# An expert layer's second bias: added by GpSimd to the block's rows instead of as a product on TensorE

## The reference, cut to what matters

```python
logits = xf @ gate_w                               # xf: layer-normed rows, 2048 x 256; 8 experts
top_w, top_idx = jax.lax.top_k(logits, TOP_K)      # TOP_K = 2
top_w = jax.nn.softmax(top_w, axis=-1)
combine = zeros((t, e)).at[arange(t)[:, None], top_idx].add(top_w)
h = jax.nn.gelu(jnp.einsum('td,edf->tef', xf, w1) + b1, approximate=False)   # f = 1024
y = jnp.einsum('tef,efd->ted', h, w2) + b2
out = jnp.einsum('ted,te->td', y, combine)
return x + out
```

## Time and profile before

| | |
|---|---|
| median of 3 runs | 340.61 us (339.21 to 341.54) |
| the profiled execution | 339.56 us, of which the trace's span is 337.7 us |
| TensorE busy | 310.3 us, 92% of the span |
| VectorE, ScalarE, GpSimd busy | 255.1, 234.3 and 173.4 us |
| products of the bias, L1261 | 39 |
| fetches L498 and stores L505 | 39 each |

### The profile page before, as it was taken

How to read it: one execution, slowest core, us unless ns; L and a number is a source line. 1 busy time by engine, 2 the same in 40 slices (tenths; PEclk the granted TensorE clock), 3 DMA queues, 4 the chain that set the end, 5 groups by cost and what they waited for, 6 DMA issues and landing times.

```text
span 337.7 us, 11884 instructions
## 1 busy us (share of the span) xinstructions
PE 310.3 (92%) x4065; PEld 286.4 (85%) x4065; DVE 255.1 (76%) x577; ACT 234.3 (69%) x537; POOL 173.4 (51%) x189
## 2 busy tenths in 40 slices
PE   7688898999899998999999999999999999999960
PEld 4678787898788897998999999999999999999950
DVE  8799998877878978786877778878777766666620
ACT  1589898982626787877778878788788665656530
POOL 6978989974142353534444444444444444443311
PEclk9999999999979999999999999999999999999995
DMA  7999999999610297888787877897879788888321
GB/s 245 289 380 337 328 353 357 327 395 364 239 39 14 47 299 205 236 233 264 185 265 204 258 219 231 245 262 213 246 231 243 232 233 237 225 256 225 95 31 16
DMA packets 49219, 78.56 MB, mean 233 GB/s; under 512 B 12117, under 2 KB 25625, under 8 KB 47114
## 3 DMA queue, kind: packets, MB, share of 16 engines
q1 hardware_dynamic: 39208, 66.72, 55.4%
q0 software_dynamic: 7600, 10.48, 20.2%
q10 hardware_dynamic: 2354, 0.59, 0.8%
HBM read 31.07 MB, written 9.64 MB: 121 GB/s over the span
## 4 chain that ended last, share of the span: by engine, by line
PE 67%; DVE 7%; issue 4%; DMA 3%; POOL 2%; ACT 1%; POOLq 1%; DVEq 0%; ACTq 0%
PE bank L1244 27%; PE bank L1259 26%; PE bank L1188 2%; PE bank L1047 2%; PE bank L1088 1%; DMA shared<-xn_rows,row_of 1%; DVE shared L1003 1%; PE bank L1106 1%; DMA out<-shared,row_of 1%; PE bank L1261 1%; DVE W L954 1%; PE bank L1063 1%; PE bank L1097 1%; PE bank L1175 1%; PE bank L1202 1%
## 5 line engine op out<-in xcount | busy, mean ns | idle before, releaser
L1259 PE MATMUL bank<-W,shared 128*128 (+1 forms) x936 | 108.7, 273 | 0.7 <-DVE shared L1026 0.7
L1244 PE MATMUL bank<-shared,XR 128*128 128x128 f16 x1680 | 99.5, 219 | 2.0 <-issue 1.8
L1244 PEld LDWEIGHTS bank<-shared,XR 128*128 128x128 f16 x1680 | 96.1, 98 | 3.9 <-issue 3.4
L1259 PEld LDWEIGHTS bank<-W,shared 128*128 128x128 f16 x936 | 89.9, 98 | 10.8 <-issue 1.1
L498 POOL DMA_INDIRECT shared<-xn_rows,row_of x39 | 40.9, 1049 | 91.0 <-DVE w_of L1019 72.2
L505 POOL DMA_INDIRECT out<-shared,row_of x39 | 61.8, 1584 | 49.9 <-ACT shared L658 27.4
L649 ACT ACTIVATE shared<-shared 128x512 f32<-128x512 f32 x78 | 49.0, 628 | 47.0 <-DVE shared L1003 33.6
L1026 DVE SCALAR_TENSOR_TENSOR shared<-shared,XP 128x512 f16<-128x512 f32 x70 | 52.3, 748 | 25.9 <-ACT shared L651 13.8
L1003 DVE SCALAR_TENSOR_TENSOR shared<-bank,XP 128x512 f32<-128x512 f32 x70 | 52.4, 748 | 20.2 <-PE bank L1244 11.9
L651 ACT ACTIVATE shared<-shared,XP 128x512 f16<-128x512 f32 x70 | 50.5, 722 | 2.3
L954 DVE SCALAR_TENSOR_TENSOR W<-W,wscale (+1 forms) x32 | 40.9, 1281 | 2.2 <-issue 1.5
(11 more groups left out here) (179 smaller groups left out, 389.2 us busy)
## 6 DMA issues: line engine op xcount, KB each, us to landing
XR<-W SPq DMA_DIRECT2D x140, 256.0 KB
W<-in_w SPq DMA_DIRECT2D x16, 1024.0 KB, 8.1
shared<-in_ctx_t SPq DMA_DIRECT2D x16, 256.0 KB, 4.8
W<-in_ctx SPq DMA_DIRECT2D x16, 128.0 KB, 6.1
out<-XR SPq DMA_DIRECT2D x16, 128.0 KB, 6.3
xn_rows<-W SPq DMA_DIRECT2D x16, 128.0 KB, 6.7
XR<-in_x SPq DMA_DIRECT2D x3, 512.0 KB, 6.2
shared<-xn_rows,row_of POOLq DMA_INDIRECT x39
```

Source lines behind the costliest of these rows:

```text
L1244: mm = pe.matmul(pHT[n][m][:, f % 4, :], first[:, c, w, f * P:(f + 1) * P], XT[:, n, v, c, :], start=(c == 0 and w == 0 and v == 0), stop= ...
L1259: pe.matmul(pY[n], hT[:, n, v, f, :], whole(Wh[:, slot, at:at + D]), start=(f == 0 and w == 0 and v == 0), stop=False)
```

## The change

Three things. The second biases no longer pass through TensorE: for each block SyncE loads the expert's bias row, repeated over 128 partitions in DRAM (`b2_rows`, 128 KB), into `XB[:, b % 3]`. GpSimd multiplies it by the token weight and by the expert's scale, which is now a 19th parameter (`YSC`), into `term`, and adds `term` to `Y` ahead of the store. To know the expert of each block, the steps are taken for a second table `expert`, beside `wslot`. `B2`, `B2s`, `y_scale` and ScalarE's `biases` are gone; `BP` holds the attention's row alone. And `keep_busy` behind the table runs 28 products, no longer 38.

```diff
+            def load_bias(b):                                   # SyncE
+                e = bass.ds(sp.value_load(expert[0:1, b:b + 1], min_val=0, max_val=E - 1), 1)
+                after(sp, term_ok, b - 2)
+                sp.dma_start(XB[:, b % 3, :], b2_rows[e].rearrange("e p d -> p (e d)")).then_inc(xb_in[b % 3], 16)
...
+            sp.wait_ge(expert_ok, 1)
+            for b in range(3):
+                load_bias(b)
             for b in range(4, NB):
...
                     sp.wait_ge(pick_ok, b - 2)
+                    sp.wait_ge(term_ok, b - 2)
                 sp.dma_start(XP[:, b % 3, :], slot_par[:, s, :].rearrange("p a x -> p (a x)")).then_inc(par_in[b % 3], 16)
+                if b == 4:
+                    load_bias(3)
+                load_bias(b)
...
             for i in range(-2, NB + 2):                         # GpSimd
                 b = i + 2
...
                         .then_inc(xg_ok[b % 3], 16)
+                b = i
+                if 0 <= b < NB:
+                    pool.wait_ge(xb_in[b % 3], 16 * (b // 3 + 1))
+                    pool.wait_ge(got_w, b + 1)
+                    if b < 4:
+                        pool.wait_ge(param_ok, 1)
+                    else:
+                        pool.wait_ge(par_in[b % 3], 16 * par_uses(b))
+                    after(pool, sum_ok, b - 2)
+                    pool.tensor_scalar(term[:, b % 3, :], XB[:, b % 3, :], w_of[:, b:b + 1], params_of(b)[:, YSC:YSC + 1],
+                                       ALU.mult, ALU.mult).then_inc(term_ok, 1)
                 b = i - 2
                 if 0 <= b:
+                    pool.wait_ge(ys_ok, b + 1)
+                    pool.wait_ge(term_ok, b + 1)
+                    pool.tensor_tensor(Y[:, b % 2, :], Y[:, b % 2, :], term[:, b % 3, :], ALU.add).then_inc(sum_ok, 1)
                     after(pool, added, 16 * b)
-                    pool.wait_ge(ys_ok, b + 1)
+                    pool.wait_ge(sum_ok, b + 1)
                     pool.indirect_dma_start(out=out,
...
-            def biases(src, dst):                               # ScalarE
-                act.activation(B2s[0:3, dst, :], B2[0:3, src, :], ACT.Copy, scale=y_scale[0:3, src]).then_inc(b2_ok, 1)
...
-            dve.memset(B2[:, :, :], 0.0).then_inc(bias_zero, 1)
-            dve.memset(B2s[:, :, :], 0.0).then_inc(bias_zero, 1)
+            dve.memset(BP[:, :], 0.0).then_inc(bias_zero, 1)
...
+                beside(dve.tensor_tensor(step_e[:, 2, 0:E - 1], permf[:, 2:E + 1], permf[:, 1:E], ALU.subtract))
...
+                for n in range(2):
+                    dve.tensor_scalar(passed[:, n, :], iotaB128[:, :], step_p[:, 0:1], step_p[:, n + 1:n + 2],
+                                      ALU.is_ge, ALU.mult).then_inc(passed_ok, 1)
...
+                        dve.tensor_scalar(wslot[:, :], pSlot[:, 0, :], float(SPARE), None, ALU.add).then_inc(wslot_ok, 1)
+                        dve.tensor_scalar(expert[:, :], pSlot[:, 1, :], permf[:, 1:2], None, ALU.add).then_inc(expert_ok, 1)
...
-            keep_busy(pIdle, 38)                                # TensorE
+            keep_busy(pIdle, 28)
...
-                    pe.wait_ge(b2_ok, min(b // 4 + 1, E))
...
-                    pe.matmul(pY[n], ones3[:, :], B2s[:, slot, :].rearrange("p a d -> p (a d)"),
-                              start=False, stop=True).then_inc(y_ok, 1)
+                    mm.then_inc(y_ok, 1)
```

More of the change, by code:

```diff
@@ L23, in after, with xattn_moe_kernel @@
         eng.wait_ge(sem, value)
-def xattn_moe_kernel(nc, x, ctx_in, ctx_t, q_rows, ck, vcol, bias9, gate, w1, b1x, w2, out):
+def xattn_moe_kernel(nc, x, ctx_in, ctx_t, q_rows, ck, vcol, bp_row, b2_rows, gate, w1, b1x, w2, out):
     T, _, D = x.shape
@@ L102, in xattn_moe_kernel @@
         CX = early(NV, D)
-        bias_rows = early(D)[0:E + 1]
-        bias_rest = early(D)[0:E + 1]
-        bias_part = early(3 * D // 2)[0:E + 1].bitcast(BF16).rearrange("e (r d) -> e r d", r=3)
+        bias_rows = early(D)[0:1]
+        bias_rest = early(D)[0:1]
+        bias_part = early(3 * D // 2)[0:1].bitcast(BF16).rearrange("e (r d) -> e r d", r=3)
         GROUP = 8
@@ L160, in xattn_moe_kernel @@
         notri = sb("notri", [P, P], BF16)
+        term = sb("term", [P, 3, D])
         ones3 = sb("ones3", [P, P], BF16)
-        B2 = sb("B2", [P, E + 1, D], BF16)
-        B2s = sb("B2s", [P, E + 1, D], BF16)
+        BP = sb("BP", [P, D], BF16)
+        XB = sb("XB", [P, 3, D])
         GW = sb("GW", [P, C, E])
@@ L201, in xattn_moe_kernel @@
         ends = sb("ends", [P, E])
-        step_e = sb("step_e", [P, 2, E])
-        step_p = sb("step_p", [P, 2])
-        passed = sb("passed", [P, NB])
+        step_e = sb("step_e", [P, 3, E])
+        step_p = sb("step_p", [P, 3])
+        passed = sb("passed", [P, 2, NB])
         wslot = sb("wslot", [P, NB], I32)
+        expert = sb("expert", [P, NB], I32)
         tv = sb("tv", [P, NB])
@@ L263, in xattn_moe_kernel @@
         v_ok, ohr_ok, table_mm, tok_ok = sem("v_ok"), sem("ohr_ok"), sem("table_mm"), sem("tok_ok")
-        passed_ok, slot_mm = sem("passed_ok"), sem("slot_mm")
+        passed_ok, slot_mm, expert_ok = sem("passed_ok"), sem("slot_mm"), sem("expert_ok")
         perm_ok, wslot_ok, comb_ok, comb_out = sem("perm_ok"), sem("wslot_ok"), sem("comb_ok"), sem("comb_out")
         comb_step, den_ok = sem("comb_step"), sem("den_ok")
-        high_ok, low_ok, param_ok, b2_ok = sem("high_ok"), sem("low_ok"), sem("param_ok"), sem("b2_ok")
+        high_ok, low_ok, param_ok = sem("high_ok"), sem("low_ok"), sem("param_ok")
+        xb_in = [sem(f"xb_in{n}") for n in range(3)]
+        term_ok, sum_ok = sem("term_ok"), sem("sum_ok")
         gelu_set = sem("gelu_set")
@@ L1085, in attended @@
                         pe.wait_ge(bias_placed, 16 * 3)
-                    pe.matmul(pO, ones3[:, :], B2[:, E, :], start=True, stop=False)
+                    pe.matmul(pO, ones3[:, :], BP[:, :], start=True, stop=False)
                     for h in range(NH):
@@ L1210, in first_of_block_0 @@
                         mm.then_inc(h_ok, 1)
-                pe.wait_ge(passed_ok, 1)
-                pe.matmul(pSlot, ones32[:, :], passed[:, :], start=True, stop=True).then_inc(slot_mm, 1)
+                pe.wait_ge(passed_ok, 2)
+                pe.matmul(pSlot, ones32[:, :], passed[:, :, :], start=True, stop=True).then_inc(slot_mm, 1)
             for i in range(-1, NB + 1):
```

30 lines of the change are left out of this document (11 added, 19 removed).

## The result

The changed kernel takes 395.41 us (median, 395.09 to 406.75), beside 341.08 us for the kernel before in the same runs: 1.160 times as long (95% interval 1.154 to 1.166). Single executions of every kernel now and then run some per cent longer at a lower granted clock, here the one of 406.75; they are left out of all ratios. The forecast was 364, range 346 to 384: slower, as forecast, but by 54 us where 25 were forecast. The profiled execution took 395.52 us (span 393.7); it is compared with before's (339.56, span 337.7).

The account below looks back on a forecast made before the run. TensorE was full; the change makes it wait on GpSimd's fetch chain, 9.28 us plus 3.5 landing, 12.8 per two periods. With start and tail, +24.7 us on 339.56 gives 364, range 346 to 384.

Parts of the forecast that it names:

- The order of GpSimd's queue: GpSimd, from w_of to the next fetch: term, addition and store now stand between, 4.72 us forecast, 0.75 before.
- The two-period sum, its first term: T(k), TensorE starting block k+1's transposes, to w_of(k) written: 4.56 us of a chain of 12.8 per two periods.
- L, the landing of the fetch: From the start of GpSimd's fetch until its rows are in: 3.5 us taken, bounds 2.8 and 4.8.
- The waits: TensorE at L1188 waits for fetched rows in nearly every mid-loop block, 0.5 to 1.3 us; period 6.1 to 6.7.
- The start: Block 0's term waits for `expert` and its load; block 3's fetch starts at 111.7, T(2) about 114.7, 3.1 us later.
- The tail: Last additions stand between ScalarE's rows and the stores: one addition and its gaps, 0.8 us, on the path.
- L1261: The 39 bias products removed from TensorE: 3.8 to 4.2 us in all, while TensorE is what ends last.
- Ten unread products: Fewer on TensorE behind the table: 0.1 to 0.6 us gained, 0.3 taken, as block 0's transposes need a fetch.
- SyncE and the DMA engines: Added 128 KB load per block: 0.8 to 1.0 us on SyncE against 1.1 of waiting; DMA 5.1 of 6.4 us.
- The first: Rival: fetches stay in time and TensorE remains the bound, 337 us; chance 0.09.
- The second: Rival: DMA engines become the bound and weights land late, period near 5.7, about 343 us; chance 0.06.
- The third: Rival: GpSimd and the fetch are slower beside VectorE, period 7.1, about 388 us; chance 0.12.

Follow-up runs that it names:

- Experiment 1: Changed kernel with GpSimd's term taken for block i-1 in iteration i, no longer block i: 351.35 us, 1.032 of the kernel before.
- experiment 3: Kernel before with only GpSimd's wait for w_of(i) put ahead of its store, no term, addition or load: 348.07 us, 1.022.
- experiment 6: Kernel before with TensorE's register load of the weights' slot moved ahead of the wait for fetched rows: 338.22 us, 0.992.
- Experiment 2: Changed kernel with TensorE's register load of the weights' slot moved ahead of the wait for fetched rows: 379.37 us, 1.114 of the kernel before.
- Experiment 7: Kernel before without the 39 bias products L1261, second biases left out: 338.54 us, 0.994.
- experiment 4: Kernel before with 28 unread products behind the table in place of 38: 339.33 us, 0.999.
- experiment 13: Changed kernel with bias rows loaded for blocks 0 to 2 only: 394.41 us, 1.162 of the kernel before.
- experiments 9 and 10: Changed kernel, term of block i-1, register load ahead, without GpSimd's arithmetic: 9 keeps SyncE's loads, 351.33 us; 10 has loads for three blocks only, 335.23.
- experiment 11: Changed kernel, term of block i-1, register load ahead, loads for three blocks; GpSimd's arithmetic behind the store, addition to an unread tile: 339.28 us, 0.994.

## Why the prediction was wrong

The sign, the chain and the place of the first wait were right. By the prediction's own steps:

*The order of GpSimd's queue.* Right. w_of to fetch is 4.60 (4.72 was forecast), partly by luck: the single costs were off in ways that cancel. The costliest groups of the changed kernel (count, busy us, mean ns):

```profile
L1053 DVE SCALAR_TENSOR_TENSOR shared<-shared,XP 128x512 f16<-128x512 f32 x70 | 60.4, 863 | 25.6 <-ACT shared L675 25.4
L528 POOL TENSOR_SCALAR term<-XB,w_of,XP 128x256 f32<-128x256 f32 x35 | 30.9, 883 | 54.3 <-issue 53.6
...
L534 POOL TENSOR_TENSOR shared<-shared,term 128x256 f32<-128x256 f32 x39 | 30.0, 769 | 0.0
```

The term takes 883 ns (0.65 us was taken, below the 0.74 of the prediction's own slope and without a reason), the addition 769 (0.70), but the last gap 0.30 us (0.75). Experiment 1 undoes the order and takes 44 us; experiment 3 shows a part of it with the wait alone.

*The two-period sum, its first term.* This step failed. "T(k) to w_of(k), 4.56 us" was read in a block in which TensorE had not waited, and used for the blocks that wait. Behind a wait it is 5.71, and 5.67 in the mean of 15, and the trace of before had shown why: the wait at 128.82 is followed by a product only at 129.98 (experiment 6). While TensorE still works on older products, the register load behind them is hidden; when it has nothing left, 0.6 to 1.1 us are on the path. Experiment 2 takes it out: 16 us in all, 14 of them between T(4) and T(36). That stretch takes 226.2 us instead of the forecast 202.4 (14.1 a pair instead of 12.8): 23.8 of the 31 us that the forecast lacked.

*L, the landing of the fetch.* Mis-sized by less: 3.66 in the block shown, 3.92 in the mean of the 15 pairs (3.3 to 5.2), where 3.5 was taken. Over the loop that is some 6 us of the 23.8.

*The clock.* The prediction had no term for it. Three stretches of 3.4 us at half clock can cost the loop 5 us at most (an estimate: what is done in them would have taken half the time at the full clock); no experiment takes them out alone, and in experiment 2 two are left.

*The waits.* "Nearly every block, 0.5 to 1.3 us" did not come: every second block waits, for longer, and the periods alternate instead of lying between 6.1 and 6.7.

*The start.* T(2) was right to 0.1 us, by luck: the fetch started at 110.97 and not at 111.7, took 1.78 us to issue instead of 0.99, and was in after 3.66 us, where the forecast left 3.0. The products behind T(2) at half clock were not seen, and T(4) is 1.65 late.

*The tail.* "0.8 on the path" was mis-sized: 5.5. The addition was costed, and not that the term of block 38 keeps back the store of block 36, so that two stores instead of one run one behind the other. The forecast for T(37) to the end was 25.56 + 0.8 - 0.3 = 26.1, measured 31.1.

The sum of the misses: 1.65 + 23.8 + 0.6 (the last period) + 5.0 = 31 us, and 362.4 + 31.1 = 393.5, measured 393.7.

*L1261.* 4.2 us were counted. Experiment 7 gives 2.2, since TensorE was nearer to its chain than the profile's full 40 us let one think. It made no difference to this result.

*Ten unread products.* 0.3 us was taken; experiment 4 can tell no difference (0.997 to 1.002), nor could it tell 0.3 from nothing.

*SyncE and the DMA engines.* "It stays in time" held in the changed kernel (37.5 us of waiting for TensorE in 23 blocks, experiment 13) for a reason that was not given: the blocks had become longer. In blocks of 5.5 us it is wrong: SyncE's room goes from 24.5 to 2.0 us and the loads cost some 17 (experiments 9 and 10). The room was added up and set against an issue of 0.8 to 1.0 us, with no allowance for blocks with less room than the mean.

*Rivals.* The first (fetches in time) and the second (DMA engines) fell: the DMA share went down. The second has some truth in experiment 1's kernel, where it is 0.86 and TensorE waits for XR. The third gave 388 and came nearest in number, but not by its mechanism, which is real and small: VectorE's low parts go from 748 to 863 ns (experiment 11 with 10: 906). The rule of the Trainium skill quoted with it (GPSIMD Engine Reference, 1. Specifications) is borne out in that. But GpSimd's stretching was offset by the short gap, and L did not come near 4.8 in the mean. As for the fetch itself, the estimate of 2.3 us from the Trainium skill (DMA: Bandwidth & Descriptors, Anatomy of one DMA) is below each one that TensorE waited for in the changed kernel, 3.0 us in the quiet start and 3.3 to 5.2 in the loop. The time that the prediction worked out for it, 346, does not fit its own bounds either: a sum of 11.6 gave 344 there.

Open: how much of the loss, up to those 5 us and what the start lost, the half clock is, and why it follows one wait and not another; and the 3 us of the arithmetic's presence, which lie at the edge of what was measured.

## What to carry to other kernels

When an added instruction waits, read what stands behind it on its queue: here the wait put 4.6 us ahead of a fetch that TensorE needed, and one line's order was 44 of 55 us. When an engine is forecast to wait where it did not, take its durations from a block of the trace in which it did wait: what it used to hide, here a register load of 1 us, comes out once in each such block. An added DMA takes time on its issuing queue as well as bytes; here a queue with 1 us of room a block in the mean had none for 1 us more.

## What was not expected of the hardware

With a register load from SBUF on TensorE behind a wait, 0.6 to 1.1 us passed until the next product in the loop of the changed kernel, and moving it ahead of the wait gained 16 us of 395 and 2.7 of 341. Behind an idle time of about 3 us TensorE's granted clock was 0.5 for 3.4 us, in three blocks of the loop and not in others with an idle time as long. A load of 128 KB by SyncE, with its register load, added 1.05 us to the time between its neighbours (2.08 against 1.03), and over 39 blocks 11 us stayed when its bytes were cut to an eighth and 6 went.
